# Attention's first steps: the values' bank and who takes them, the order of the normalisations and of the queries' copy, the place of the squares

## The reference

```python
# layer 0: y = act_quant(val * gelu(gate)) @ weight_quant(down).T + x
def attention(x, W_q, W_k, W_v, W_o):          # 16 heads of 16
    q, k, v = split(x @ W_q.T), split(x @ W_k.T), split(x @ W_v.T)
    attn = softmax(0.25 * einsum('bnqd,bnkd->bnqk', q, k), axis=-1)
    return join(einsum('bnqk,bnkd->bnqd', attn, v)) @ W_o.T
# layer 1
h = gamma(cond) * rmsnorm(x) + beta(cond)
x = x + alpha(cond) * attention(h, W_q, W_k, W_v, W_o)
x = x + alpha2(cond) * swiglu(gamma2(cond) * rmsnorm(x) + beta2(cond), ...)
# layer 2: an adapter whose weights are made from cond; layer 3: a layer norm
```

## Time and profile before

| | us |
|---|---|
| median of 3 runs (741.74 to 741.99) | 741.75 |
| the profiled execution's own time | 741.11 |
| its span | 739.3 |
| PE busy | 721.8 (98%) |
| DVE busy | 514.7 (70%) |
| POOL busy | 410.6 (56%) |
| ACT busy | 359.3 (49%) |

### The profile page before, as it was taken

One profiled execution on the slowest core, in us unless ns is written; L12 is line 12 of the kernel. 1 busy time (PEld: TensorE's weight loads), 2 busy tenths in 40 slices (PEclk: granted clock), 3 DMA queues, 4 the chain that ended last, 5 costly groups with the idle time before them and its releaser, 6 DMA issues.

```text
span 739.3 us, 18704 instructions
## 1 busy us (share of the span) xinstructions
PE 721.8 (98%) x6700; PEld 586.4 (79%) x6700; DVE 514.7 (70%) x808; ACT 359.3 (49%) x722; POOL 410.6 (56%) x408
## 2 busy tenths in 40 slices
PE   9999999999999899999999999999999999999996
PEld 8888888888888788888888777777777767778884
DVE  4977777777789989888995465656655566453466
ACT  4534444344447677888874333333333332322585
POOL 5645655554678888999997624224242423320244
PEclk9999999999999999999999999999999999999999
DMA  8854544445432000000004255577667777759943
GB/s 301 258 111 99 108 121 101 100 111 121 110 73 63 22 28 17 17 1 0 1 4 134 104 173 175 177 220 216 191 190 251 212 215 231 238 160 390 386 178 142
DMA packets 81339, 106.25 MB, mean 144 GB/s; under 512 B 39904, under 2 KB 53376, under 8 KB 81152
## 3 DMA queue, kind: packets, MB, share of 16 engines
q1 hardware_dynamic: 79840, 103.34, 46.7%
q10 hardware_dynamic: 1440, 2.11, 1.1%
HBM read 75.77 MB, written 21.27 MB: 131 GB/s over the span
## 4 chain that ended last, share of the span: by engine, by line
PE 75%; POOL 16%; issue 5%; DVE 3%; ACT 1%; DMA 0%; POOLq 0%; DVEq 0%; SPq 0%; ACTq 0%
PE banks L446 24%; PE banks L1317 22%; PE banks L1347 12%; POOL p_sb L1047 5%; PE banks L1369 4%; PE banks L530 4%; POOL mlp_in L182 2%; PE banks L1979 2%; PE banks L1949 2%; POOL mlp_in L186 2%; POOL x_sb L1056 2%; POOL att_in_lo L191 1%; PE banks L1971 1%; POOL mlp_in L188 1%; PE banks L548 1%
## 5 line engine op out<-in xcount | busy, mean ns | idle before, releaser
L629 ACT ACTIVATE gelu<-banks,rstd 128x512 f32<-128x512 f32 x64 | 44.0, 688 | 115.8 <-PE banks L446 114.1
L1699 DVE TENSOR_TENSOR g<-banks,silu 128x512 f32<-128x512 f32 x64 | 44.2, 690 | 77.6 <-PE banks L1317 44.9
L1703 DVE TENSOR_TENSOR g_lo<-g,g_hi 128x512 fp32r<-128x512 f32 x64 | 55.7, 870 | 47.6 <-ACT g_hi L1539 47.6
L1539 ACT ACTIVATE g_hi<-g 128x512 fp32r<-128x512 f32 x64 | 40.4, 631 | 96.0 <-DVE g L1699 95.0
L1533 ACT ACTIVATE silu<-banks 128x512 f32<-128x512 f32 x64 | 38.2, 597 | 97.4 <-PE banks L1317 97.4
L446 PE MATMUL banks<-up_hi,xs_hi 128*128 128x512 f32 x254 | 81.1, 400 | 0.0
L446 PE MATMUL banks<-up_hi,xs_lo 128*128 128x512 f32 x256 | 79.2, 391 | 0.0
L1317 PE MATMUL banks<-mlp_in_hi,w_hi 128*128 128x512 f32 x252 | 78.8, 394 | 0.0
L446 PE MATMUL banks<-up_lo,xs_hi 128*128 128x512 f32 x256 | 78.8, 390 | 0.0
L1317 PE MATMUL banks<-mlp_in_lo,w_hi 128*128 128x512 f32 x252 | 78.0, 390 | 0.0
L1317 PE MATMUL banks<-mlp_in_hi,w_lo 128*128 128x512 f32 x252 | 77.8, 390 | 0.0
(11 more groups left out here) (230 smaller groups left out, 1736.2 us busy)
## 6 DMA issues: line engine op xcount, KB each, us to landing
gen_hyper<-in_gen_t SPq DMA_DIRECT2D x32, 512.0 KB, 4.4
gen_made<-base_w SPq DMA_DIRECT2D x64, 256.0 KB, 4.4
adapter_w<-gen_made SPq DMA_DIRECT2D x64, 256.0 KB, 4.4
tokens<-in_x_tok SPq DMA_DIRECT2D x32, 128.0 KB, 2.3
w_stage<-in_w_t SPq DMA_DIRECT2D x32, 128.0 KB, 2.6
tokens_again<-in_x_tok SPq DMA_DIRECT2D x32, 128.0 KB, 2.2
weight_slot<-adapter_w SPq DMA_DIRECT2D x4, 1024.0 KB, 8.8
x_sb<-in_x_t SPq DMA_DIRECT2D x7, 512.0 KB, 6.3
```

Source lines behind the costliest of these rows:

```text
L629: nc.scalar.activation(gelu[:, j, :], up_bank(s, j, 1)[:, :], ACT.Gelu, scale=rstd0[:, bass.ds(s.at(0), 1)]).then_inc(Z["gelu_done"], 1)
L1539: nc.scalar.activation(gs[0][:, f % 2, :], g[:, f % 2, :], ACT.Copy).then_inc(S["g_hi_done"], 1)
L1699: nc.vector.tensor_tensor(g[:, f % 2, :], chunk_bank(s, f, 1)[:, :], silu[:, f % 2, :], ALU.mult).then_inc(S["g_done"], 1)
L1703: nc.vector.tensor_tensor(gs[1][:, f % 2, :], g[:, f % 2, :], gs[0][:, f % 2, :].bitcast(FP32), ALU.subtract).then_inc(S["g_ready"], 1)
```

## The change

Values always go to bank 0. PE's `keys` wait only for the copies of the keys before them, `values` wait for the scaled output (from step 4 on) or for the copies of the values before them, and `output` waits in all steps from 4 on (the two last ones apart) for the copies of the values made in the step before. ACT takes all four pieces of the values in steps 3 to 8. POOL's `normalise` moves ahead of `attention_input` part 2 in steps 3 (both halves) and 4 (the first half); the second half of step 4 moves ahead of `residual`. ACT's `take_queries` of step 3 moves ahead of the second exponentials. PE's `squares` move behind the queries.

```diff
         def value_sums(s, member, parity):
-            rows = bank[0 if s.first_tile(2) or s.first_tile(3) or plain(s) else 1][L * member:L * (member + 1), :]
+            rows = bank[0][L * member:L * (member + 1), :]
...
         def vector_takes_values(s):
-            return not plain(s) or s.last(2)
+            return s.first_tile(2) or s.last(2)
...  POOL
+                first_two = s.first_tile(3) or s.first_tile(4)
...
+                    if first_two:
+                        normalise(s, 0)
                     if s.first_tile(3):
-                        normalise(s, 0)
+                        normalise(s, 1)
                     wait(pool, A["v_ready"], s.at(1) if s.live(2) else 0)
                     attention_input(nc, pool, core, s, 2)
+                    if s.first_tile(4):
+                        normalise(s, 1)
                     if not plain(s):
                         residual(s)
-                if not s.first_tile(3):
+                if not first_two:
                     normalise(s, 0)
-                normalise(s, 1)
+                    normalise(s, 1)
...  PE keys
-                    if s.first_tile(3):
+                    if s.live(2):
                         pe.wait_ge(A["k_done"], s.at(1))
-                    elif s.live(2):
-                        pe.wait_ge(A["v_low_done"], s.at(1))
-                        pe.wait_ge(A["v_high_done"], s.at(1))
...  PE values
-                k, apart = s.slot(1, 2), s.first_tile(1) or s.first_tile(2) or before_plain(s)
-                if before_plain(s):
+                k = s.slot(1, 2)
+                if s.live(4):
                     pe.wait_ge(A["ya_done"], s.at(4) + 1)
-                elif not apart:
-                    pe.wait_ge(A["k_done"], s.at(1) + 1)
+                elif s.live(2):
+                    pe.wait_ge(A["v_low_done"], s.at(1))
+                    pe.wait_ge(A["v_high_done"], s.at(1))
...
-                            last = nc.tensor.matmul(bank[0 if apart else 1][:, pair * D:(pair + 1) * D],
+                            last = nc.tensor.matmul(bank[0][:, pair * D:(pair + 1) * D],
...  PE output
-                    if plain(s) and not s.last(3) and not s.last(4):
+                    if not s.last(3) and not s.last(4):
                         pe.wait_ge(A["v_low_done"], s.at(2) + 1)
                         pe.wait_ge(A["v_high_done"], s.at(2) + 1)
...  PE attention_body
-                squares(s)
                 keys(s)
                 queries(s)
+                squares(s)
                 weighted_values(s)
...  ACT attention_body
                 take_transposed(s, 1)
+                if s.first_tile(3):
+                    take_queries(s)
                 if first_two:
                     exponentials(s, 1)
-                if s.first_tile(3):
-                    take_queries(s)
```

## The result

The changed kernel takes 745.99 us (median of 5 runs, 745.56 to 746.64) against 741.74 us (5 runs): +4.25 us, a ratio of 1.0062 with an interval of 1.0051 to 1.0073. The forecast was 744.3 with a range to 745.5: the right side, by the mechanism that was named, and 1.7 us too little. Measured again on another chip it was 745.98 against 741.6 (1.0052, 1.0039 to 1.0066).

The account below looks back on a forecast made before the run. POOL's chain was taken to bound attention. The profiled 741.11 us plus 1.4 (start gain and step 5 stall) and 1.15 (slow clock) gave 743.7; the median, 0.64 above that execution, was forecast at 744.3, range 742.8 to 745.5.

Parts of the forecast that it names:

- POOL is the bound and a shift of it arrives whole: Attention, steps 3 to 9: POOL runs almost without gaps, so its shift reaches the kernel's end in full.
- A period other than 10.62: Sign of being wrong: POOL's steps 6 to 8 last something other than 10.62 us each.
- The start of the chain, gain 0.66: Step 3: DVE without value copies starts subtracting 0.78 us earlier, so POOL's L182 of step 4 comes 0.66 us earlier.
- The residual late by 3.08 us, the queue behind the square, POOL waiting 2.9 us: Steps 4 and 5: ACT's square waits for the late residual, delaying queued work; POOL waits 2.9 us before L191, previously 0.87.
- PE's gap and its clock, +1.15: Step 5: a 5.2 us PE gap halves the clock, costing between 0 and 2.3 us; the middle, 1.15, was taken.
- Steps 6 to 8 carried, 0: Steps 6 to 8 and the loop: extra ACT copies and shorter PE waits don't reach POOL; 0 us.
- rival D: Slow clock outlasts step 5's second transposes and makes step 6 late too: up to +4.2 us, 746; chance 0.10.

Follow-up runs that it names:

- the last version: Changed kernel with squares one step later, queries' copy back, POOL's old step 4, residual ahead of L191 and earlier DVE scaling in steps 5 to 8: 740.27 us.
- residual first: Changed kernel, but in step 4 POOL does the residual ahead of the second normalisation: 743.33 us.
- clock kept in step 5 only: Changed kernel with 14 unread matmuls of ones on PE before step 5's output product, none in step 4: 743.8 us.
- the later square: Changed kernel with POOL's new order kept, but ACT makes each square one step later, behind the second copy of transposes: 741.78 us.
- both gaps filled: Changed kernel with unread matmuls of ones in PE's gaps of steps 4 and 5: 743.17 us, and 743.76 us in a later job.

## Why the prediction was wrong in size and right in kind

- *POOL is the bound and a shift of it arrives whole*: right in the main. POOL's shift at step 9 is that of the kernel's median within 0.6 us in every run but the last version, where it is 2.65 us against 1.1. In the changed kernel steps 6 and 7 are the old 10.6 us, but step 8 is 10.95 (295.15 to 306.10). A period other than 10.62 was named as a sign of being wrong, and this one appeared.
- *The start of the chain, gain 0.66*: 0.41 measured. The first normalisation of step 3 came 0.60 us earlier in place of 0.78, since the transposes and the subtraction behind them each came about 0.1 later than laid out. And the order is not free, as the prediction took it to be: with POOL's old order the gain at step 4's L182 is 0.62, and POOL's new order alone makes it 0.19 late.
- *The residual late by 3.08 us, the queue behind the square, POOL waiting 2.9 us*: right. Without the slow clock the wait is 3.02 and 3.01.
- *PE's gap and its clock, +1.15*: this step failed. That the clock falls in step 5 was right, and nearly so the gap (4.66 us in place of 5.2; 5.09 where the clock stays up in step 4). Its price was not: the low clock held until the second transposes were done. The output product took 1.22 us more and they 0.40, and 1.65 us came due, where I took the middle of 0 and 2.3. And a second fall was missed. The forecast looked at one gap only; the gap of 1.75 us in step 4, which the queries' move opens by running the scores early, was priced at nothing, since only gaps beyond 4 us were thought to matter. Together 2.0 to 2.2 us in place of 1.15.
- *Steps 6 to 8 carried, 0*: nearly. POOL waits 1.15 us in step 8 in place of 0.87, 0.28 more, in the changed kernel and in all experiments with its value copies and the old place of the residual. ACT is idle then and starts L198 0.37 us after its input is there, where it took 0.1 in the other steps. What holds it is not shown, and was not tried.
- The sum by these terms: -0.41 + (3.02 - 0.87) + 1.65 + 0.34 + 0.28 = 4.0, against 4.25 measured; the other 0.2 is not placed. Of POOL's 4.0 the forecast had 2.55. The clock is some 0.84 of what it lacked, step 8 0.28, the start 0.25 and the stall 0.1; the clock alone would have left the time inside the range. The range was too narrow at its upper end: rival D was given 0.10 and the second fall nothing.

The Trainium skill, "TensorE: Matmul & The Clock Gate", section "HAM oscillation — how this bites in real kernels", was drawn on for the fall of the clock after a long wait. By that rule, the traces agree for step 5 (4.66 us of gap). The falls after 1.75 us stand in them too, and the rule as it was drawn on, for a long wait, would not have given those.

## What to carry to other kernels

When work is put ahead of an instruction, look at who waits for that instruction and what is queued behind the waiter. A late residual was harmless (741.78 us) or cost 4 us, depending on where its one reader stood in its queue. Price every PE gap that an edit opens, short ones too, with half speed for the whole product behind it. And time given to engines off the chain (0.9 us of DVE work, 0.5 to 0.7 us of PE waits) moved POOL by 0.6 us at the start and the kernel by nothing that can be measured (741.75 us with POOL's old order), while filling POOL's own 0.87 us of idle brought the only gain in time.

## What the runs showed of the hardware that I had not expected

The granted clock fell after a gap of 1.75 us in all five traces that have it (the changed kernel twice, residual first, clock kept in step 5 only, POOL's old order), and after 2.83 and 3.22 us. It did not fall after 2.03 us (the later square, step 6) nor after 1.77 us (both gaps filled, step 5). Nor did it after 1.48 us (the later square, step 4). So the gap's length alone doesn't tell, and what else decides was not taken apart. Behind the gaps of 1.75 us the fall came 0.25 to 0.7 us after PE had resumed; in the gap of 4.66 us it came 2.0 us into it, and after the 3.22 us 1.5 us behind its end. In the changed kernel the clock came back 4.2 us after PE had resumed (262.01 to about 266.2), and with the queries' copy back 6.1 us after (260.63 to about 266.7).
